# Rows of v made by TensorE for the first two groups of a language-model tower, with k ahead of v in the opening

## What is computed

```python
h = tok_ref(x, ...)                      # embedding + 0.1 * (W_proj[d] @ W_exp[d] @ base) for the token's domain d
qkv = layernorm(h) @ Wqkv.T + b          # q, k, v: 16 heads of 16 channels; k = k / sqrt(16)
retention = 1 - sigmoid(Lambda_raw)      # (16 heads, 16, 16)
def step(state, qkv_t):
    hebbian = einsum('bhi,bhj->bhij', v_t, k_t)
    state = retention * state + Gamma * hebbian
    y_t = einsum('bhij,bhj->bhi', W_static + state, q_t)
    return state, y_t
h = h + y @ out_w.T + out_b
h = h + quantized_ffn(layernorm(h))      # per-token and per-channel rounding to 8 bits
```

## Time and profile before

| | us |
|---|---|
| median of 3 runs | 252.12 |
| lowest, highest | 250.42, 253.32 |
| the profiled execution | 251.63 |
| its span in the trace | 249.8 |
| TensorE (PE) busy | 222.4 (89%) |
| VectorE (DVE) busy | 195.7 (78%) |
| GpSimd (POOL) busy | 190.4 (76%) |
| ScalarE (ACT) busy | 108.0 (43%) |

### The profile page before, as it was taken

How to read it: one execution, slowest core, us unless ns; L and a number is a source line. 1 busy time by engine, 2 the same in 40 slices (tenths; PEclk the granted TensorE clock), 3 DMA queues, 4 the chain that set the end, 5 groups by cost and what they waited for, 6 DMA issues and landing times.

```text
span 249.8 us, 7732 instructions
## 1 busy us (share of the span) xinstructions
PE 222.4 (89%) x3218; PEld 163.5 (65%) x3218; DVE 195.7 (78%) x389; ACT 108.0 (43%) x272; POOL 190.4 (76%) x100
## 2 busy tenths in 40 slices
...
GB/s 155 138 254 133 42 87 192 149 45 42 38 129 87 272 72 46 45 1 45 179 145 21 104 152 3 0 46 175 134 35 99 155 3 4 1 87 3 0 0 84
DMA packets 19442, 21.24 MB, mean 85 GB/s; under 512 B 2416, under 2 KB 13904, under 8 KB 19408
## 3 DMA queue, kind: packets, MB, share of 16 engines
...
...
## 4 chain that ended last, share of the span: by engine, by line
PE 69%; DVE 15%; issue 5%; ACT 4%; DMA 3%; POOL 3%; SPq 0%; DVEq 0%; ACTq 0%; POOLq 0%
PE y_ps L1157 10%; PE scr L1005 10%; PE w_ps L1137 9%; PE scr L982 6%; PE y_ps L1099 5%; PE scr L995 5%; PE scr L1019 5%; PE scr L1034 4%; PE scr L959 4%; DVE zz L923 3%; POOL uu L473 3%; PE scr L1072 2%; PE scr L1058 2%; PE y_ps L1148 2%; PE y_ps L1043 2%
## 5 line engine op out<-in xcount | busy, mean ns | idle before, releaser
L473 POOL TENSOR_TENSOR uu<-vg,kk 128x1024 f32<-128x1024 f32 x64 | 151.3, 2405 | 28.3 <-DMA vg<-v_far 19.1
L923 DVE TENSOR_TENSOR zz<-e_hg,q_ps 128x1524 f32<-128x1524 f32 x31 | 53.6, 1728 | 0.0
L892 DVE TENSOR_TENSOR_SCAN e_hg<-decay,w_ps 128x512 f32<-128x512 f32 x32 | 38.9, 1217 | 10.4 <-PE w_ps L1137 9.8
L1137 PE MATMUL w_ps<-uu,comb 128*32 128x128 f32 x1024 | 36.7, 284 | 1.4 <-POOL uu L473 1.1
L1157 PE MATMUL y_ps<-zz,coll 128*32 128x128 f32 x768 | 28.9, 284 | 6.3 <-DVE zz L923 6.3
L1137 PEld LDWEIGHTS w_ps<-uu,comb 128*32 128x32 f32 x1024 | 28.8, 114 | 8.6 <-issue 7.4
L1157 PEld LDWEIGHTS y_ps<-zz,coll 128*32 128x32 f32 x768 | 20.4, 112 | 20.3 <-issue 9.5
L553 ACT ACTIVATE junk<-tok_dom 128x256 bf16<-128x256 f32 x24 | 9.7, 407 | 28.6 <-DVE tok_dom L690 28.6
L909 DVE TENSOR_TENSOR zz<-e_hg,q_ps 128x512 f32<-128x512 f32 x32 | 21.7, 678 | 0.0
L401 POOL DMA_INDIRECT tok_dom<-in_table,ids_sb x16 | 15.5, 969 | 6.2 <-issue 3.5
L415 POOL TENSOR_TENSOR tok_dom<-tok_dom,bf 128x1024 f32<-128x1024 f32 (+1 forms) x5 | 9.0, 1791 | 13.7 <-ACT tmp_b L578 11.8
...
## 6 DMA issues: line engine op xcount, KB each, us to landing
...
tok_dom<-in_table,ids_sb POOLq DMA_INDIRECT x16, 4.3
...
```

What stands on the lines that cost most here:

```text
L473: pool.tensor_tensor(uu[:, g % NU, two], v_of.to_broadcast(shape), k_of.to_broadcast(shape), ALU.mult).then_inc(s_u, 1)
L892: dve.tensor_tensor_scan(states(g).rearrange("p a m -> p (a m)"), decay[:, NA * n:NA * (n + 1)].rearrange("p a m -> p (a m)"), w.rearrange ...
L923: dve.tensor_tensor(z, e.to_broadcast(shape), q.to_broadcast(shape), ALU.mult).then_inc(s_z, 1)
L1137: last = pe.matmul(w_ps[32 * hp:32 * hp + 32, g % NW, a], comb[:, NA * n + a, hp], uu[:, g % NU, hp, a], start=True, stop=True, skip_group ...
```

## The change

For the groups 0 and 1 (`DIRECT = 2`) the rows of v no longer go by HBM. The host lays the columns of v's weights out repeated (`w_rows`, 256 KB), with the bias repeated likewise (`b_rows`, 4 KB). A new stage `v_rows` on TensorE makes each group's rows with 32 matmuls of the form that k uses (weights 128 x 32, 128 columns), and ScalarE evacuates them with four instructions of 128 x 128 straight into `vg`. POOL waits for that instead of the DMA. SyncE issues no DMA for these two groups, and loads the two new tensors behind bk. v itself (`v_sb`) is still made, since `gv` and the other groups need it. The five tables are written anew: in the opening and in chunk 1 k stands ahead of v, in chunks 2 and 3 v stays ahead of k, and other stages move by a few slots.

```diff
+DIRECT = 2
 PE_CALENDAR = """
-    wake 0.8, xhat_t 0.1, wake 0.3, v 0.0, k 0.0, q 0.0, v 0.1, k 0.1, base_t 1.0, q 0.1; 0: dom 1.0; 2: base_t 1.1,
+    wake 0.8, xhat_t 0.1, wake 0.3, k 0.0, v_rows 0.0, v 0.0, v_rows 0.1, q 0.0, k 0.1, v 0.1, q 0.1; 0: base_t 1.0,
...
 ACT_CALENDAR = """
...
-    0.0, xhat 0.1, xhat_t 0.1, bo_hi 0.0, w_round 0.0, v 0.0, bo_mid 0.0, b_scale 0.0, k 0.0, bo_lo 0.0, q 0.0, v 0.1,
-    k 0.1, q 0.1; 3: base_t 1.0, domain 1.0; 4: dom 1.0; 5: base_t 1.1, w_t 0.0; 6: moments1 1.0; 7: w_t 0.1; 8:
+    0.0, b_scale 0.0, xhat 0.1, xhat_t 0.1, bo_hi 0.0, k 0.0, v_rows 0.0, v 0.0, v_rows 0.1, w_round 0.0, bo_mid 0.0,
+    q 0.0, bo_lo 0.0, k 0.1, v 0.1, q 0.1; 1: base_t 1.0; 4: domain 1.0, dom 1.0; 5: base_t 1.1; 6: moments1 1.0, w_t
...
+        bv_rows = sb("bv_rows", [P, DIRECT, NA])
+        wv_rows = sb("wv_rows", [P, KD, DIRECT, NA, 32])
...
-            for dst, src in ((wv, w_v), (bv, b_v), (wk, w_k), (bk, b_k), (wq, w_q), (bq, b_q)):
+            for dst, src in ((wv, w_v), (bv, b_v), (wk, w_k), (bk, b_k), (wv_rows, w_rows), (bv_rows, b_rows), (wq, w_q),
+                             (bq, b_q)):
...
             def rows_v(g):
 
+                if g < DIRECT:
+                    return
                 c, n, hg, b = group(g)
-                if b == 0:
+                if b == 0 or g == DIRECT:
                     sp.wait_ge(s_v4[hg], 16 * (c + 1))
...
-                        pool.wait_ge(s_vrow[g % NVG], 16 * (g // NVG + 1))
+                        if g < DIRECT:
+                            taken(pool, "v_rows", 0, g)
+                        else:
+                            pool.wait_ge(s_vrow[g % NVG], 16 * (g // NVG + (g % NVG >= DIRECT)))
...
             def b_scale(*_):
-                act.wait_ge(s_w_qkv, 96)
+                act.wait_ge(s_w_qkv, 128)
...
+            def v_rows(_, g):
+
+                bank = filled(act, "v_rows", 0, g)
+                for a in range(NA):
+                    last = act.activation(vg[:, g, a], scr[:, bank, MB * a:MB * (a + 1)], ACT.Identity,
+                                          bias=bv_rows[:, g, a:a + 1])
+                last.then_inc(s_free[bank], 1)
...
+            def v_rows(_, g):
+
+                bank = scratch("v_rows", 0, g)
+                pe.wait_ge(s_w_qkv, 128)
+                for a in range(NA):
+                    for k_ in range(KD):
+                        for o in range(BLK):
+                            last = pe.matmul(scr[32 * o:32 * o + 32, bank, MB * a:MB * (a + 1)],
+                                             wv_rows[:, k_, g, a],
                                              act_t[:, k_, MB * o:MB * (o + 1)], start=(k_ == 0),
                                              stop=(k_ == KD - 1), skip_group_check=True)
                 last.then_inc(s_full[bank], 1)
```

More of the change, by code:

```diff
@@ new lines @@
+    dom 1.0; 1: base_t 1.1; 2: expand 1.0; 3: expand 1.1, pair0 0.0; 4: corr 1.0; 6: pair1 0.0; 8: corr 1.1, w_t 0.0;
+    9: w_t 0.1; 13: fix 0.0; 16: xhat_t 1.0, xhat_t 1.1, w_row 0.0; 17: k 1.0; 18: v 1.0, v 1.1; 20: k 1.1; 23: pair1
+    0.1; 24: pair0 0.1; 29: q 1.0; 31: base_t 2.1, base_t 2.0; 32: fix 0.1; 34: dom 2.0, expand 2.0, expand 2.1; 38:
+    pair0 1.0; 39: corr 2.0; 41: q 1.1, corr 2.1; 42: pair1 1.0, attn 0.0; 44: xhat_t 2.0; 45: attn 0.1; 46: xhat_t
+    2.1; 48: v 2.0, v 2.1, k 2.0; 51: k 2.1; 52: xq_t 0.0; 53: fix 1.0; 55: ffn 0.0; 56: xq_t 0.1, ffn 0.1; 59: pair0
@@ new lines @@
+    1.1, pair1 1.1; 61: q 2.0; 63: base_t 3.1, base_t 3.0; 64: fix 1.1; 66: dom 3.0, expand 3.0, expand 3.1; 70: pair0
+    2.0; 71: corr 3.0; 73: q 2.1, corr 3.1; 74: pair1 2.0, attn 1.0; 76: xhat_t 3.0; 77: attn 1.1; 78: xhat_t 3.1; 80:
+    v 3.0, v 3.1, k 3.0; 83: k 3.1; 84: xq_t 1.0; 85: fix 2.0; 87: ffn 1.0; 88: xq_t 1.1, ffn 1.1; 91: pair0 2.1,
+    pair1 2.1; 93: q 3.0; 96: fix 2.1; 100: pair0 3.0; 105: q 3.1; 107: pair1 3.0, attn 2.0; 109: attn 2.1; 118: fix
+    3.0; 120: xq_t 2.0, xq_t 2.1; 121: ffn 2.0, ffn 2.1; 122: pair0 3.1; 123: pair1 3.1; 124: fix 3.1; 133: wake 3.8;
@@ L81 @@
[L81 to L85, removed]
@@ L91 @@
     -1: w_ret 0.0, mask 0.0, mask 0.1, stat1 0.0, rstd1 0.0, stat1 0.1, rstd1 0.1, w_amax 0.0, w_comb 0.0, bo_less
[L92 to L100, removed]
+    0.0, bo_less2 0.0, w_int 0.0, w_coll 0.0, w_lag 0.0; 0: mask 1.0; 1: qk 0.0; 2: gv0 0.0; 3: mask 1.1; 6: stat1
@@ L1120, in _ @@
                                      lambda c, h: pe.wait_ge(s_xhat[0], 2 * c + h + 1), idf, scr_two),
-                     "v": channel_major("v", wv), "k": k, "pair0": pair(0), "pair1": pair(1), "fix": fix,
+                     "v": channel_major("v", wv), "v_rows": v_rows, "k": k, "pair0": pair(0), "pair1": pair(1), "fix": fix,
                      "q": channel_major("q", wq), "xq_t": transposes("xq_t", lambda c, t: xq[:, t, :],
@@ L1125, in _ @@
                      "ffn": ffn, "w_t": w_t, "w_row": w_row, "wake": wake}
-            operand = {"expand": "base_t", "corr": "expand", "v": "xhat_t", "k": "xhat_t", "q": "xhat_t"}
+            operand = {"expand": "base_t", "corr": "expand", "v": "xhat_t", "v_rows": "xhat_t", "k": "xhat_t", "q": "xhat_t"}
             def combine(g):
```

51 lines of the change are left out of this document (35 added, 16 removed).

## The result

| | before | after |
|---|---|---|
| median us | 252.12 (5 runs, 250.42 to 253.32) | 263.19 (5 runs, 259.82 to 264.66) |
| the profiled execution, its span | 251.63, 249.8 | 259.82, 257.9 |

The change makes the kernel slower: ratio 1.040 (95% interval 1.034 to 1.046), 11 us, outside the predicted 250 to 258. The profiled execution of after is the shortest of its five, so the trace shows 8.1 us of span, and the other four runs are 3 to 5 us longer than the one traced.

What follows compares the result with a forecast made beforehand. TensorE was taken to set the pace, with v's HBM round trip on the chain. +0.2 (b_scale) + 3.9 (v_rows) - 0.6 (base_t) - 1.8 (idle won back) = +1.7; + 0.6 (base_t) = +2.3: 254.2 us, range 250.0 to 258.0.

Steps and rivals of the forecast that it cites:

- VectorE and the port: Opening: VectorE's tables wait till 38.35, then run unbroken until 43.45 while POOL loses 5.1 us.
- scan(0) at 46.3: VectorE's first scan, behind the tables, was to start at 46.3 instead of 42.30, at no extra cost.
- Rival 3: POOL gets in between VectorE's 12 instructions: scan(0) at 56, some 264 us; milder form 255 to 257.5; chance 0.2.
- Its threshold, 47.9: Chunk 1's mask waits for expand till 47.9; the port rival was to decide once scan(0) starts behind that.
- First product at 31.25: POOL's first product in the opening was to start at 31.25 instead of 34.55, 3.3 us earlier.
- The 0.2 for b_scale: ScalarE's b_scale, ahead of the second xhat, was to delay k's start to 26.10, adding 0.2 us.
- First combine at 42.85: End of TensorE's opening queue: first combine at 42.85, 1.7 us later than 41.16, its operands there some 5 us before.
- v to start at 38.9: TensorE's v 0.1 in the opening needs the bank that q leaves, so starts at 38.9, not 37.86.
- `v_rows` at +3.9, half won back: TensorE's opening: two added stages cost 3.9 us, with 1.8 us of idle time won back ahead of combine(0).
- transposes at 64.5: Chunk 1's transposes were to start at 64.5 instead of 62.24; an end no later would show the prediction wrong.
- +2.3 at the transposes to +2.3 at the end: Later slots were priced at 0, so the 2.3 us delay at chunk 1's transposes stays to the end.
- rival 1: Opening absorbed: 250.1 us; second part, last chunk spared a low-clock stretch, 1.8 more: 248.3; chance 0.15.

Runs made afterwards that it cites:

- w_coll at the head: The changed kernel with w_coll and w_lag moved ahead of bo_less2 and w_int on VectorE, ScalarE unchanged; 264.25 us, ratio 1.053 to before.
- the order in which the tables keep their length: The changed kernel with w_round ahead of k and bo_lo last in ScalarE's opening, bo_less2 behind w_lag on VectorE; 250.23 us, ratio 1.001 to before.
- before with two small moves: The kernel before with bo_less2 behind w_lag on VectorE and bo_lo at the end of ScalarE's opening; 250.01 us, ratio 1.001 to before.
- the kernel with the tables first: The changed kernel with w_round ahead of k on ScalarE and bo_less2 behind w_lag on VectorE; 254.91 us, ratio 1.020 to before.

## Why the prediction was wrong

The failing step is in "VectorE and the port": "a row of VectorE instructions without a gap is not broken up", hence VectorE "keeps its turn for 36.32 - 31.23 = 5.1 us". It has two faults.

First, the row in the trace of before was one where VectorE was there before POOL; I used it for the opposite case. After shows the opposite case: VectorE comes into a running row of products and gets one instruction per product, 36.7 to 45.2 for four instructions that take 0.42 + 2 x 0.24 + 0.42 = 1.3 us where POOL is made to wait. Second, even the case I had seen is not a rule, as w_coll at the head shows: 1.16 us of lead, and broken up. Three boundaries passed in one execution are one event, not three, since it was one product that was kept out.

That sentence carried the sum: scan(0) at 46.3 was measured at 53.93. Rival 3, with a chance of 0.2 and some 264, names the mechanism and was close in time (263.19). It said scan(0) at 56, by counting four products more; POOL ran dry at 45.0 for 1.38 us and then had two products only, which let four of the w_coll through. Its threshold, 47.9 for the start of scan(0), leaves out scan(0)'s own 1.2: `mask` comes behind its end, so it decides from 46.7 on, and the forecast's 46.3 stood just short of it. 53.93 lies well beyond either: `mask` started at 55.06, 7.2 behind 47.9, and all behind it moved with it. The rival's rule was the one that the prediction quotes from the Trainium skill, read narrowly; I had it beside me and set it aside.

Point by point for the rest:

- First product at 31.25: measured 30.89. Right; with k's start at 25.83 for 26.10, the 5.06 between them is as worked out (5.15). The 0.2 for b_scale did not come: k starts 0.1 us earlier than v did in before (25.91).
- First combine at 42.85: measured 41.92, and 41.81 in the kernel whose k starts 1.1 us later. The term is mis-sized: stages "at 1.96 each". From k to the next the starts lie 1.75, 1.88 and 1.92 apart (25.83, 27.58, 29.46, 31.38); a row's length holds the tail that overlaps the next stage, so the pitch is what adds up. It stated "wrong if combine(0) starts before 41.5", and in after it did not.
- "v to start at 38.9" for the bank that q leaves: measured 38.04 with 0.90 of wait for `q_ps`. The wait is there.
- `v_rows` at +3.9, half won back: the sum of the opening's TensorE, transposes at 64.5, was right for the order in which the tables keep their length (64.32). But that delay did not become time at the end: that kernel is level with before, and at chunk 2's transposes nothing is left of it (107.28 against 107.50). The prediction names this as a sign of being wrong, "transposes at 64.5 turn into an end that is no later", and it came: the step from +2.3 at the transposes to +2.3 at the end fails as well. It is not the later slots that give the delay back, since before with two small moves does it in the old ones.
- The clock in the middle was not in the sum at all. Behind the 7.69 us wait TensorE was granted 0.65 of its clock for 5.3 us: between the two levels, mostly at 1.2 GHz. L1064 and one combine took 1.62 and 1.94, where 0.88 and 1.08 are their lengths at full clock (both stand in the trace of the kernel with the tables first, 53.33 and 54.15), 1.6 us together.
- The account then closes by rows: `mask` 9.7 later, 1.6 for the clock, less some 0.8 won back, is the 10.5 at the transposes; 2.4 of it is given back by the end of the span, 1.0 in chunk 1 and 1.4 behind chunk 2's transposes, where after is spared the first of before's two stretches at the low clock. That is the second part of rival 1 (1.8 us), in a kernel that lost for another reason. My 2.3 were a part of a delay that lay wholly in the shadow of VectorE.
- The range (to 258.0) took in only rival 3's milder part. With ends of 2.4 and 9.5 us for one mechanism with a chance of 0.2, and a written rule behind the harder one, the upper end belonged nearer to it.
